# Loading the destination windows of a message pass through ACT's queue, four per tile, in place of SP's, eight per pair of tiles

## The reference

```python
def _mlp(h, W, b, gamma, beta):
    h = relu(h @ W + b)
    mu = mean(h, axis=0); var = mean(square(h - mu), axis=0)
    return gamma * (h - mu) * rsqrt(var + EPS) + beta

# layer 1, the message pass of this case
edge_feat = _mlp(edge_attr, W_edge, b_edge, g_edge, beta_edge)      # E x 96
message   = concatenate([x[row], x[col], edge_feat], axis=1)        # row: source, col: destination
message   = _mlp(message, W_msg, b_msg, g_msg, beta_msg)            # E x 96
out       = segment_sum(message, col) + node_feat
```

## Time and profile before

| | |
|---|---|
| median of 3 runs | 5566.3 us (5557.26 to 5571.82) |
| profiled execution | 5569.94 us |
| its span, first to last instruction | 5568.1 us |
| mean granted TensorE clock | 0.818 |
| message pass in it | 1600 to 3799 us |
| busy in the message pass: PE, DVE, ACT, POOL | 1071.8, 962.0, 485.9, 1312.1 us |

### The profile page before, as it was taken

How to read it: one execution, slowest core, us unless ns; L and a number is a source line. 1 busy time by engine, 2 the same in 40 slices (tenths; PEclk the granted TensorE clock), 3 DMA queues, 4 the chain that set the end, 5 groups by cost and what they waited for, 6 DMA issues and landing times.

```text
span 5568.1 us, 71606 instructions
## 1 busy us (share of the span) xinstructions
PE 3216.9 (58%) x18541; PEld 2357.2 (42%) x18541; DVE 2708.7 (49%) x6211; ACT 1578.4 (28%) x3821; POOL 2483.5 (45%) x2580
## 2 busy tenths in 40 slices
PE   0444444444464454454444445443118999999999
PEld 0333233333343333333333333332106887778877
DVE  3777777777644444444444444436313234433333
ACT  1666666666222222222222222222000001111000
POOL 6555555555555566656555655666760000000000
PEclk9999999999986666666666666655558999999999
DMA  6555555555223333333333333332014666666676
GB/s 202 168 178 181 166 180 180 170 178 168 64 73 87 87 97 89 87 87 90 86 91 84 95 88 89 85 88 54 2 44 172 248 249 247 245 249 251 254 276 231
DMA packets 411992, 801.65 MB, mean 144 GB/s; under 512 B 237480, under 2 KB 288396, under 8 KB 385692
## 3 DMA queue, kind: packets, MB, share of 16 engines
q1 hardware_dynamic: 263894, 591.99, 31.8%
q0 software_dynamic: 82320, 90.28, 7.8%
q10 hardware_dynamic: 65718, 118.62, 5.6%
HBM read 581.84 MB, written 218.74 MB: 144 GB/s over the span
## 4 chain that ended last, share of the span: by engine, by line
another core or an unknown queue 30%; PE 27%; issue 17%; ACT 12%; DVE 8%; ACTq 3%; POOL 1%; SPq 1%; DMA 0%; DVEq 0%; POOLq 0%
PE ps L991 22%; ACT ps L1040 2%; ACT dump L1044 2%; ACT out_ring L1056 2%; ACT relu_dump L1040 2%; DVE second L1474 2%; ACT second L1081 1%; PE ps L953 1%; ACT out_ring L1064 1%; ACTq L1066 1%; DVE area L1490 1%; ACT ps L1076 1%; ACTq L1060 1%; DVE second L1484 1%
## 5 line engine op out<-in xcount | busy, mean ns | idle before, releaser
L843 PE MATMUL ps<-ident,area 96*128 96x96 f32 x2352 | 441.3, 355 | 1154.6 <-ACT out_ring L1056 425.5
L693 POOL DMA_INDIRECT area<-src_table,idx_src x784 | 750.5, 957 | 525.1 <-DMA idx_src<-src_dram 270.3
L693 POOL DMA_INDIRECT area<-relu_table,idx_src x784 | 739.5, 943 | 537.3 <-issue 336.1
L843 PEld LDWEIGHTS ps<-ident,area 96*128 96x128 f32 x2352 | 352.1, 211 | 1281.3 <-issue 957.8
L1461 DVE TENSOR_TENSOR_SCAN area<-flags,area,ps 96x512 f32<-96x512 int8 x196 | 249.8, 1274 | 1213.5 <-ACT dump L1044 1007.4
L704 POOL DMA_INDIRECT adj<-copies_ring,cell_ring x587 | 578.1, 985 | 378.0 <-DVE cell_ring L1442 198.4
L991 PE MATMUL ps<-early,area 128*128 128x288 bf16 x5194 | 665.8, 287 | 1.6 <-DVE early L1606 1.6
L991 PE MATMUL ps<-second,area 128*128 128x288 bf16 x5194 | 651.2, 286 | 0.5 <-DVE second L1606 0.5
L991 PEld LDWEIGHTS ps<-early,area 128*128 128x128 f16 x5194 | 508.9, 98 | 129.8 <-issue 2.1
L991 PEld LDWEIGHTS ps<-second,area 128*128 128x128 f16 x5194 | 508.2, 98 | 128.1 <-DVE second L1606 1.1
L1426 DVE SCALAR_TENSOR_TENSOR second<-second,area,ps 128x512 bf16<-128x512 f32 x784 | 538.6, 743 | 0.0
(11 more groups left out here) (298 smaller groups left out, 4555.1 us busy)
## 6 DMA issues: line engine op xcount, KB each, us to landing
area<-adj SPq DMA_DIRECT2D x196, 1632.0 KB
adj<-early SPq DMA_DIRECT2D x102, 816.0 KB
soft_sums<-out_ring ACTq DMA_DIRECT2D x196, 384.0 KB
second<-key_dram SPq DMA_DIRECT2D x98, 512.0 KB
area<-dst_table SPq DMA_DIRECT2D x784, 48.0 KB
sums<-out_ring ACTq DMA_DIRECT2D x196, 192.0 KB
second<-caps_dram SPq DMA_DIRECT2D x98, 192.0 KB
attr<-attr_parts SPq DMA_DIRECT2D x196, 72.0 KB
```

What stands on the lines that cost most here:

```text
L693: pool.indirect_dma_start(out=src_rows[:, s, c, :], out_offset=None, in_=gather_table[p], in_offset=bass.IndirectOffsetOnAxis(ap=idx_src[s ...
L843: last = nc.tensor.transpose(ps[:, b, c * F:(c + 1) * F], r[:, (s * CH + c) * P:(s * CH + c + 1) * P], ident[0:F, 0:F])
```

## The change

The eight windows per pair leave SP's `load`. A new step of ACT, `load_windows(u, s)`, issues four per tile, at the head of `relu_features` of the same tile. It loads four registers from `first_rank`, waits for `turned` of the tile that used the same buffer before, and starts the four transfers through ACT's queue. Buffers, sizes and the consumer are unchanged.

```diff
@@ SP: load(u, h)
-                    if kind == MESSAGE:
-                        _, firsts = nc.values_load_multi_w_load_instructions(
-                            first_rank[0:1, bass.ds(t * CH, 2 * CH)], engines=[mybir.EngineType.SP], min_val=0, max_val=NP,
-                            skip_runtime_bounds_check_because="a count of runs, of which there are NP at most")
-
                     wait(sp, src_gathered[s], use * 16 * CH)
...
                                      ranks_t[one, :].to_broadcast([P, 2 * TE])).then_inc(ranks_landed[h], 16)
-
-                        for c in range(2 * CH):
-                            sp.dma_start(dst_rows[:, s + c // CH, c % CH, :], dst_table[bass.ds(firsts[c], P), :])\
-                              .then_inc(window_landed[s + c // CH], 16)
@@ ACT: relu_features(u, s)
+                def load_windows(u, s):
+                    t = u * RING + s
+                    _, firsts = nc.values_load_multi_w_load_instructions(
+                        first_rank[0:1, bass.ds(t * CH, CH)], engines=[mybir.EngineType.Activation], min_val=0, max_val=NP,
+                        skip_runtime_bounds_check_because="a count of runs, of which there are NP at most")
+                    wait(act, e["turned"], t - RING + 1)
+                    for c in range(CH):
+                        act.dma_start(dst_rows[:, s, c, :], dst_table[bass.ds(firsts[c], P), :]).then_inc(window_landed[s], 16)
+
                 def relu_features(u, s):
+                    load_windows(u, s)
                     t = u * RING + s
                     wait(act, e["hid"], t + 1)
```

## The result

The changed kernel took 5618.43 us (median of 5 runs, 5601.49 to 5627.89), the kernel before 5566.3 (5557.26 to 5572.35). The ratio is 1.0089, 95% interval 1.0065 to 1.0113: slower by 52 us. The forecast was slower too, but by 104 us.

What follows compares the result with a forecast made beforehand. POOL's queue was taken to bound the message pass. Blocks of 537 us replacing 461.7 us of waits (+75), plus +30 for late scatters, gave +105 on 5569.9, adjusted to 5670 us; range 5350 to 5930, own case 5600 to 5800.

Steps and rivals of the forecast that it cites:

- The bound and the two waits: Message pass: POOL sets the pace; only its waits for idx_src (270.3 us) and cell_ring (191.4 us) can be won.
- SP's part: SP's queue: without windows, indices are requested a pair ahead and the index wait goes, −270.3 us; no slow loads remain.
- The new wait: POOL in the message pass: without index pauses, it blocks on cell_ring after three scatters, 8.77 us per block.
- two-tile rival: POOL's runs: scores miss the early part, so POOL blocks after two scatters; +398 us, 5960, mixed 5800 to 5960; chance 0.10.
- runs of 17.8 us: Profile after, POOL's runs: if they are 17.8 us long instead of 26 to 36, the prediction is wrong.
- The sum: Message pass: 61.3 blocks × 8.77 = 537 us replace 461.7, +75; with +30 for late scatters, +105 us.
- The late third scatter: POOL's run: later hrelu delays its third scatter by 0 to 2.2 us; half a microsecond on 61 runs, +30 us.
- ACT's cost: ACT in the message pass: TENSOR_LOAD and four DMA issues take 2.8 to 3.0 us a tile, covered in the mean.
- ACT's issues stretch above 1 us: Profile after, ACT's window issues: expected at 0.33 to 0.38 us; above 1 us, the prediction is wrong.
- slow-queue rival: ACT's queue: windows cost what they did on SP, 13.0 us a tile; +349 us, 5900 and more; chance 0.05.
- Landing at nothing: PE's use of windows: the transfers' landing is nearly hidden, taken as 0, upper end 2 us per block.
- POOL freed: Rival, message pass: without SP's slow issues, held signals pass, POOL runs at 8.92 to 9.1 us a tile; 5135 to 5300; chance 0.16.

Runs made afterwards that it cites:

- redirect first, windows on SP: Kernel before, with DVE running redirect of a tile ahead of its scan and a semaphore per scatter slot: 5595.97 against 5559.48 us, ratio 1.0070.
- no windows in the loop: Changed kernel, with windows of the first four tiles loaded once and reused by later tiles: 5540.72 us against 5520.09 of the kernel before, ratio 1.0033.
- windows behind hrelu: Changed kernel, with ACT's four windows moved behind the ReLU of the features: 5600.28 us against 5527.24 of the kernel before, ratio 1.0141.
- redirect first, windows on ACT: Changed kernel, with DVE running redirect ahead of scan and a semaphore per scatter slot: 5404.43 us against 5523.52 of the kernel before, ratio 0.9785.
- chip 11: Changed kernel, unaltered, on a chip where PE's signals reach ACT at once: 4777.93 us against 4779.75 of the kernel before, ratio 0.9998.

## Why the prediction came out as it did

The whole difference lies in the message pass, and there in POOL's idle time. For each kernel, the time from the first scatter to the last, and what of it POOL wasn't busy (the busy time is 1312.3 to 1315.7 us in all six):

| kernel | before on its chip | first to last scatter | less 2202.7 | POOL idle in it | less 890.2 | measured against before |
|---|---|---|---|---|---|---|
| before | 5566 | 2202.7 | | 890.2 | | |
| changed | 5566 | 2248.5 | +46 | 936.2 | +46 | +52 |
| redirect first, windows on SP | 5559 | 2238.1 | +35 | 925.5 | +35 | +36 |
| no windows in the loop | 5520 | 2197.7 | −5 | 882.1 | −8 | +21 |
| windows behind hrelu | 5527 | 2252.6 | +50 | 940.2 | +50 | +73 |
| redirect first, windows on ACT | 5524 | 2062.1 | −141 | 746.4 | −144 | −119 |

Behind the last scatter all six need 1740.0 to 1742.4 us. On the two chips on which the kernel before takes as long as in its trace, the pass gives the measured difference to 6 us. The three others are 22 to 26 us under it, all alike. The kernel before takes 39 to 46 us less on those chips, so its pass may be shorter there as well; no trace of it on them shows this.

- *The bound and the two waits:* right on the two chips that can be compared with the trace, and not contradicted on the three others.
- *SP's part:* right. The index wait went to nothing, −270 us, and the time did not follow it. Slow loads remain on SP, though, which the prediction ruled out: at 2446.77 the index load took 0.73 us, inside a run of POOL.
- *The new wait:* right in kind. "Blocks every three tiles" is what the kernel without windows does, 65 of 65.3. The changed kernel does something else: two tiles in 53 of 81 runs. That is the two-tile rival, which I had given 0.10, in two thirds of the runs, and "runs of 17.8 us" was my own sign of being wrong. It costs little because a pause after two tiles is 5.4 us and not 8.77. That POOL's index waits "were pauses too" is shown from the other side by redirect first on the kernel before.
- *The sum:* this is the step that failed. The mechanism was right, and the term "61.3 blocks × 8.77 us = 537" was too high; with the +30 it made 567 us of waits, where 520.9 were measured, and +105 in place of +59. I took 8.77 us from a single block in the timeline. The row of the kernel before had 24 of them in 191.4 us, 7.98 each; the blocks of the kernel without windows, which has nothing else, are 65 of 7.39, 480 us. The one run in five with a fourth tile, which brought 65.3 blocks down to 61.3, isn't there: that kernel has none, the changed one 2 of 81. That 65.3 × 7.98 is 521 us, just what the changed kernel waits, is luck, since it has 83 waits of 6.28.
- *The late third scatter, 0 to 2.2 us a run:* wrong in its mechanism. Where that scatter's signal misses, the scatter is late by a whole pause, 3.3 to 7.0 us, and POOL's run is over after two tiles. Against this stands the shorter pause, and ACT's windows add 41 us to POOL's wait (520.9 against 480.1 in the kernel without them) and 31 us to the time. My +30 comes near this by luck.
- *ACT's cost, 2.8 to 3.0 us a tile:* 2.5 where quick; TENSOR_LOAD took 310 ns, not 691. But the mean of a group of four is 2.78 us, where on chip 11 it is 1.86, and one took 12.60. "ACT's issues stretch above 1 us" was a sign of being wrong too. So the slow-queue rival had a share, which I had put aside on the rows of the store; no run prices it alone.
- *Landing at nothing:* right as far as the matmuls that wait for windows show; the weight load at L822, the first to need one, waited 6.9 us in 15 pieces for them. The profile puts 224.4 us of PE's waits at L816 down to `dst_table`, but that matmul waits for `hrelu`, behind ACT's windows.
- *POOL freed:* it did not happen with signals held; where they are not held, the kernel before takes the same time as the changed one, whose trace is free of these waits, so it must be nearly free of them too.

What stays open: why PE's signals are held on some chips and not on others, and whether POOL's back-to-back issuing slows SP or only goes along with it. The kernel before was the same on all of them, and no run here tells it apart. Nor was it tried on a chip with held signals whether moving the windows behind `hrelu` helps once redirect is first.

## What to carry to other kernels

A long wait in the profile may be doing another wait's work: ask, before removing it, what comes through while the engine stands still, and which wait asks for that pause next. Price a repeating wait by the row that groups all its pieces, not by one that looks typical, and price its length and its number together: here more pauses came out shorter. Where two waits trade with each other, edit both: each edit alone was a loss here (+0.9% and +0.7%), together they gained 2.15%.

## What the runs showed of the hardware that was not expected

- The same kernel takes 4780 to 4785 us on some chips and 5520 to 5566 on others. Where the traces were compared, POOL's instructions take the same time (0.94 to 1.0 us), and what differs is PE's signals and issues and SP's issues while POOL issues indirect DMAs back to back: 0.12 us from a score's end to ACT against 16 to 20, and a median of 3.98 us against 11.1 for SP's eight windows.
- ACT, whose 196 stores never took over 374 ns, shows issues of up to 1392 ns once it carries 784 window loads among the same runs of POOL, and single groups of four of up to 12.60 us. On chip 11 no group took over 2.99 us.
- TENSOR_LOAD of four registers on ACT took 310 ns in the median, of eight on SP 691.
